# A decoder layer on one Trainium2 core: projection weights in three pieces, a new order of the first block, and another row length for the folded keys

## The chip, the cores and the metric

The kernel runs on 1 core of one Trainium2 chip, as one launch. The metric is the time on the device in microseconds (us); lower is better. The core has TensorE (PE, matrix products, into PSUM banks), VectorE (DVE), ScalarE (ACT), GpSimd (POOL) and SyncE (SP), which here only issues transfers. Each engine takes its own instructions in order, and a semaphore wait holds up all that is behind it on that engine.

## The reference

One pre-norm decoder layer for 8 sequences of 256 tokens of width 256, in float32:

```
x = x + attn(layernorm(x))      # 16 heads of 16, rotary Q and K, causal softmax, W_o
x = x + xattn(layernorm(x))     # 16 heads of 64 over 77 context rows, masked softmax, W_O
x = x + ffn(layernorm(x))       # 256 -> 1024 -> 256, gelu, 8-bit fake-quantised weights + LoRA of rank 16
```

In the cross attention K = ctx @ W_K and Q = xn @ W_Q, and scores = Q K^T / 8. The mask takes context rows out.

## The kernel before, in words

The 8 sequences are blocks 0 to 7. All of the code is unrolled. Each engine has a list of calls written out by hand (`keys(0, 0)`, `project(1, 0)`, ...), which mixes the stages of up to three blocks; the meeting points are semaphores inside the called functions.

Every product with float32 accuracy is made of three matmuls: each operand is split into a high part (ACT copies it to the rounded type) and a low part (raw minus high, on DVE or POOL), and PE makes hi x hi, hi x lo, lo x hi. So each weight passes through a load, `split_hi` on ACT and `split_lo` on DVE or POOL before PE can use it. Each activation passes through PE, ACT and DVE likewise.

Stages of self attention for block a: `statistics_a`, a power on POOL (`inverse_deviation`), `norm_a`, `transpose_a`, `xaT_part` (both halves of the split), `project(a, 0)` and `project(a, 1)` for Q and K, `project_v(a)`, `rotary` on DVE and `rotate` on POOL, `rotated` on ACT, then through DRAM (`store_rotated`, `stacks`) into q_stack and k_stack. `scores(a, g)` for 8 groups of two heads and `maxima` on DVE find each row's maximum. It is transposed (`transpose_max`, `maxima` on ACT into mnegT) and stored by SP (`shifts(a, half)`) into two rows of q_stack, so that `shifted(a, g)` gives scores less the maximum. `exponentials`, `causal` on POOL, `weigh`, `turn_a`, `turn_back_a`, `output_a` follow. Groups 4 to 7 need `shifts(a, 1)`.

Cross attention doesn't make Q. In the prologue the kernel folds W_Q into the keys of all 8 blocks at once: for m = 0 to 7 (two heads each) `keys(m, half)` makes the keys (PE, then ACT and DVE split them, then PE goes on), `fold_keys(m, k, half)` multiplies them with W_Q^T, ACT and DVE copy the result to `stage[m % 2]`, and `store_fold(m)` writes it to `fold_dram` with two transfers of 616 KB. `values2(t, half)` makes the values of all blocks, which POOL stores to v2_dram. Later, for each block b and each group g of four heads, `load_fold(b, g)` brings 308 KB back, ACT and POOL split it (`fold_hi`, `fold_lo`), and `scores2(b, g)` uses it. There are two slots, so a load waits for the scores2 of two groups before.

Before: `fold_dram` is [block, group, k, 128, 308]. A store writes, for each of 128 partitions and 8 blocks, 154 numbers (616 bytes) in one run. A load reads 256 rows of 308 numbers (1232 bytes).

The start: POOL fills the constants, v_aug, k_stack and `work` (ones), all ahead of the first power, and `shift_rows` on SP waits for them all (const_ok 8) ahead of the loads of W_K, ctx and W_Q. W_q, W_k and W_v of self attention are loaded by three transfers and split as one.

Of the kernel before, what the change touches and what calls it, by code (L numbers as in the profile page):

```python
# [21 lines left out]
P = 128  # L22
# [16 lines left out]
def decoder_layer(nc, x, ctxT, mask, wqT, wkT, wvT, woT, wQT, wK, wV, wO, wfcT, bfc, Afc, BfcT,  # L39
# [24 lines left out]
    with ExitStack() as ctx:  # L64
# [111 lines left out]
        fold_dram = nc.dram_tensor("fold_dram", [NB, H // GH, KD, P, GW], F32, kind="Internal").ap()  # L176
# [7 lines left out]
        trig_ld, const_ld, const_ok, ones_ld = sem("trig_ld"), sem("const_ld"), sem("const_ok"), sem("ones_ld")  # L184
        weights = ("qkv", "ctx", "wk", "wv", "wo", "fc", "pj", "wo2", "wq")
# [60 lines left out]
        RAW_DMAS = [3, 1, 1, 1, 1, 1, 1, 1, 1]  # L246
# [13 lines left out]
        def _(sp):  # L260
# [3 lines left out]
            def weight(k):  # L264
                if k == QKV_W:
                    load_raw(sp, k, *[(tiles(k, 3 * D)[:, :, j * D:(j + 1) * D], rows(w))
                                      for j, w in enumerate((wqT, wkT, wvT))])
                elif k == FC_W:
# [28 lines left out]
            def store_fold(m):  # L297
# [3 lines left out]
                for k in range(KD):  # L301
                    sp.dma_start(fold_dram[:, g, k, :, c * 2 * S2:(c + 1) * 2 * S2].rearrange("b p n -> p b n"),
# [59 lines left out]
            def load_fold(b, g):  # L362
# [48 lines left out]
            weight(WO2_W)  # L411
            stacks(1, 0)
            lora_columns()
            stacks(1, 1)
            load_fold(0, 2)
            context_values(0)
            load_fold(0, 3)
            store_rotated(2)
            load_fold(1, 0)
            weight(FC_W)  # L420
            residual_input(1)
            load_x(3)
            biases()
            shifts(1, 0)
            load_fold(1, 1)
            shifts(1, 1)
            stacks(2, 0)
            load_mask(1)
            stacks(2, 1)
            store_rotated(3)  # L430
            residual_input(2)
            load_x(4)
            shifts(2, 0)
            load_fold(1, 2)
            context_values(1)
            load_fold(1, 3)
            load_mask(2)
# [69 lines left out]
        def _(pool):  # L507
            pool.memset(ident[:], 0.0)
# [31 lines left out]
            def split_lo(k):  # L540
                pool.wait_ge(w_hi[k], 1)
# [253 lines left out]
        def _(pe):  # L795
# [79 lines left out]
            def transpose_a(a):  # L875
                if isinstance(a, int) and a == 0:
                    pe.wait_ge(const_ok, 7)
# [2145 lines left out]
```

## Time and profile before

| | us |
|---|---|
| median of 3 timed runs | 632.96 |
| the runs | 632.96, 637.38, 631.59 |
| the profiled execution | 640.39 |
| its span | 638.6 |
| PE busy | 528.9 (83% of the span) |
| DVE, ACT, POOL busy | 394.3, 301.3, 249.0 |

The rows further down are of the profiled execution. Times in them are us from the start of the span, unless marked ns.

### The profile page before, as it was taken

How to read it: one execution, taken by the hardware profiler on the slowest of the kernel's cores; microseconds unless marked ns; L12 is line 12 of the kernel's file. 1: busy time of each engine (PE TensorE's matmuls, PEld its weight loads, DVE VectorE, ACT ScalarE, POOL GpSimd, SP SyncE). 2: the span in 40 equal slices, each digit the busy share in tenths (PEclk: the TensorE clock that was granted, in tenths of full speed). 3: DMA queues.
4: the chain of work that ended last, by engine and by line, in shares of the span. 5: the costliest groups of instructions: out<-in, count | busy, mean ns of one | idle time of the engine just before them, and what ended most of it. 6: DMA issues, size and time to landing. Idle time of an engine off the chain costs nothing.

```text
span 638.6 us, 11817 instructions
## 1 busy us (share of the span) xinstructions
PE 528.9 (83%) x4334; PEld 449.0 (70%) x4334; DVE 394.3 (62%) x1093; ACT 301.3 (47%) x484; POOL 249.0 (39%) x317
## 2 busy tenths in 40 slices
PE   2488779877987889889988997899899899957955
PEld 2376666665867767878778776878887687846755
DVE  4657622488867963796388548954983683554332
ACT  2323344432362765166535654663556277426323
POOL 5820021455256355155252526272465016522210
PEclk9779986987797999999999999999999999989969
DMA  5598997966040414051315232325140601111000
GB/s 186 167 233 174 193 216 143 225 218 205 26 100 1 150 34 121 1 160 52 88 49 147 61 83 72 89 60 118 37 112 19 157 22 42 37 41 38 1 16 17
DMA packets 63709, 62.45 MB, mean 98 GB/s; under 512 B 6868, under 2 KB 60804, under 8 KB 63652
## 3 DMA queue, kind: packets, MB, share of 16 engines
q1 hardware_dynamic: 62148, 56.74, 34.8%
q0 software_dynamic: 1504, 4.95, 2.2%
q8 instruction: 35, 0.57, 0.4%
q14 instruction: 22, 0.18, 0.1%
HBM read 38.28 MB, written 23.10 MB: 96 GB/s over the span
## 4 chain that ended last, share of the span: by engine, by line
PE 54%; DVE 23%; ACT 8%; issue 5%; DMA 5%; POOL 3%; SPq 1%; DVEq 0%; ACTq 0%; POOLq 0%
PE banks L798 9%; PE banks L799 8%; PE banks L800 8%; PE banks L958 5%; DVE banks L2382 4%; PE banks L1049 4%; PE banks L1060 4%; PE banks L935 4%; PE banks L1122 2%; DMA x_in<-in_x 2%; PE banks L972 2%; ACT probs L1752 2%; DMA fold_raw<-fold_dram 2%; DVE hid_lo L2337 2%; PE banks L832 1%
## 5 line engine op out<-in xcount | busy, mean ns | idle before, releaser
L2382 DVE CUSTOM_DVE_ANT_0 banks<-banks,causal_qk 128x256 f32<-128x256 f32 (+1 forms) x256 | 84.1, 388 | 13.0 <-PE banks L935 11.2
L582 POOL TENSOR_SCALAR_AFFINE_SELECT probs<-probs 128x256 f32<-128x256 f32 x128 | 52.2, 435 | 70.1 <-ACT probs L1752 70.1
L565 POOL TENSOR_TENSOR work<-work,rc 128x616 f32<-128x616 f32 x32 | 40.5, 1266 | 99.7 <-DVE rc L2482 99.7
L1752 ACT ACTIVATE probs<-banks 128x768 f32<-128x768 f32 x64 | 51.7, 808 | 32.5 <-PE banks L958 31.8
L1720 ACT ACTIVATE work<-banks 77x512 f32<-77x512 f32 (+1 forms) x72 | 43.2, 600 | 48.4 <-PE banks L1049 44.0
L572 POOL TENSOR_TENSOR fold_lo<-fold_raw,fold_hi 128x616 fp32r<-128x616 f32 x32 | 48.6, 1523 | 43.4 <-ACT fold_hi L1720 43.4
L2480 DVE TENSOR_REDUCE sm<-work 128x8 f32<-128x616 f32 x32 | 25.4, 793 | 51.0 <-ACT work L1782 50.9
L935 PE MATMUL banks<-k_stack,q_stack 96*128 96x256 f32 (+1 forms) x256 | 42.0, 288 | 13.0 <-DVE mneg L2382 9.7
L958 PE MATMUL banks<-q_stack,k_stack 100*128 100x128 f32 (+1 forms) x256 | 47.1, 309 | 5.7 <-DMA q_stack<-mnegT 2.7
L935 PEld LDWEIGHTS banks<-k_stack,q_stack 96*128 96x128 f32 x256 | 36.2, 197 | 20.2 <-DVE mneg L2382 11.6
L2337 DVE TENSOR_TENSOR late<-banks,late 128x512 fp32r<-128x512 f32 x40 | 27.4, 684 | 35.0 <-ACT late L1720 35.0
L1122 PE MATMUL banks<-late,wfc_hi 128*128 128x256 f32 x256 | 42.4, 296 | 6.6 <-DVE up_x L2337 3.4
L798 PE MATMUL banks<-fold_hi,xbT_hi 128*128 128x308 f32 x128 | 47.7, 372 | 0.0
L958 PEld LDWEIGHTS banks<-q_stack,k_stack 100*128 100x128 f32 x256 | 35.9, 201 | 15.2 <-ACT probs L1752 7.5
L1049 PE MATMUL banks<-ident,work 128*77 128x128 f32 x256 | 41.0, 284 | 6.6 <-ACT work L1720 3.0
L1720 ACT ACTIVATE late<-banks 128x512 fp32r<-128x512 f32 x40 | 23.8, 595 | 41.3 <-PE banks L1060 25.5
L1810 ACT ACTIVATE wfc_raw<-banks,bfc_t,wscale 128x256 f32<-128x256 f32 x64 | 32.0, 561 | 20.5 <-DVE hid_lo L2337 15.1
L1122 PEld LDWEIGHTS banks<-late,wfc_hi 128*128 128x128 f32 x256 | 36.1, 197 | 7.7 <-DVE up_x L2337 4.2
L799 PE MATMUL banks<-fold_lo,xbT_hi 128*128 128x308 f32 x128 | 40.1, 314 | 0.0
L800 PE MATMUL banks<-fold_hi,xbT_lo 128*128 128x308 f32 x128 | 39.9, 312 | 0.0
L798 PE MATMUL banks<-wo_hi,late 128*128 128x256 f32 x128 | 39.4, 308 | 0.2 <-DVE late L2337 0.2
L798 PE MATMUL banks<-wpj_hi,hid_hi 128*128 128x256 f32 x128 | 37.7, 295 | 1.8 <-ACT wfc_raw L1810 1.0
(190 smaller groups left out, 1574.7 us busy)
## 6 DMA issues: line engine op xcount, KB each, us to landing
fold_raw<-fold_dram SPq DMA_DIRECT2D x32, 308.0 KB, 3.1
fold_dram<-work SPq DMA_DIRECT2D x8, 616.0 KB, 8.5
rot_dram<-rot_s_hi SPq DMA_DIRECT2D x16, 256.0 KB, 3.0
rot_dram<-rot_s_lo SPq DMA_DIRECT2D x16, 256.0 KB, 2.8
q_stack<-rot_dram SPq DMA_DIRECT2D x32, 128.0 KB, 2.7
k_stack<-rot_dram SPq DMA_DIRECT2D x32, 128.0 KB, 3.0
fold_dram<-fold_raw SPq DMA_DIRECT2D x4, 616.0 KB, 6.1
fold_dram<-fold_raw_hi SPq DMA_DIRECT2D x4, 616.0 KB, 8.4
```

Of the source, the lines that this page charges most:

```text
L572: pool.tensor_tensor(fold[1][:, :, g % 2], raw[:, :, g % 2], fold[0][:, :, g % 2].bitcast(F32), ALU.subtract).then_inc(g_lo, 1)
L582: last = pool.affine_select(out=diagonal, in_=diagonal, compare_op=ALU.is_ge, fill=0.0, base=0, pattern=[[0, 2], [1, P]], channel_multipli ...
L798: pe.matmul(dst, w[0], x_[0], start=first, stop=False, **kw)
L799: pe.matmul(dst, w[0], x_[1], start=False, stop=False, **kw)
L800: return pe.matmul(dst, w[1], x_[0], start=False, stop=last, **kw)
L935: mm = pe.matmul(halves(banks[p])[:, 1 - q, 0:keys_q], q_stack[0:BOTH, g, q * P:(q + 1) * P], k_stack[0:BOTH, g, p, 0:keys_q], start=(q == ...
L958: mm = pe.matmul(halves(p)[:, 1 - k, k * P:T], k_stack[0:SX, g, p, k * P:(k + 1) * P], q_stack[0:SX, g, k * P:T], start=(k == 1), stop=(k ...
L1049: mm = pe.transpose(bank[0:S2, 5, p * T + q * P:p * T + (q + 1) * P], sc2[g % 2][:, q, 2 * c + p, :], ident[:])
L1122: pe.matmul(dst, wfc[0][:, k, m * P:(m + 1) * P], xfT[piece][:, k, :], start=(k == 0 and piece == 0), stop=False)
L1720: act.activation(dst, src, ACT.Copy).then_inc(done, 1)
L1752: act.activation(probs[:, n:n + 2, :], bank[:, 0:2, P:4 * P], ACT.Exp, scale=SCALE).then_inc(p_ok, 1)
L2382: last = dve.tensor_tensor_reduce(out=held[:, at], in0=held[:, at], in1=bias, scale=-1.0, scalar=HUGE, op0=ALU.add, op1=ALU.min, accum_out ...
```

## The change

1. W_q, W_k, W_v of self attention: three transfers with a semaphore each (qkv_ld), split piece by piece (`projection_hi` on ACT, `projection_lo` on DVE); `project(0, 0)`, `project(0, 1)` and `project_v(0)` wait for one, two and three pieces.
2. POOL's fills: half_a comes first, then ident, the causal mask and half of k_stack. The other half, the ones (now 2 partitions) and v_aug come behind the first power, with semaphores of their own. `shift_rows` waits for these, and stands behind the load of W_Q. The low part of W_Q moves from POOL to DVE.
3. `fold_dram` is [group, k, 128, c, block, 154]: a store writes one run of 4928 bytes for each partition, a load reads 512 rows of 616 bytes with two transfers.
4. New orders on all engines, up to about the middle of block 1.

```diff
-        fold_dram = nc.dram_tensor("fold_dram", [NB, H // GH, KD, P, GW], F32, kind="Internal").ap()
+        fold_dram = nc.dram_tensor("fold_dram", [H // GH, KD, P, 2, NB, 2 * S2], F32, kind="Internal").ap()
...
+            def projection(j):
+                sp.dma_start(tiles(QKV_W, 3 * D)[:, :, j * D:(j + 1) * D],
+                             rows((wqT, wkT, wvT)[j])).then_inc(qkv_ld[j], 16)
+
             def shift_rows():
-                sp.wait_ge(const_ok, 8)
+                sp.wait_ge(stack_zero, 2)
+                sp.wait_ge(ones_set, 1)
...
                 for k in range(KD):
-                    sp.dma_start(fold_dram[:, g, k, :, c * 2 * S2:(c + 1) * 2 * S2].rearrange("b p n -> p b n"),
+                    sp.dma_start(fold_dram[g, k, :, c],
                                  stage[m % 2][k].rearrange("p b a s -> p b (a s)")).then_inc(fold_st[m % 2], 16)
...
-                sp.dma_start(raws["fold"][:].rearrange("p (k g n) -> p k g n", k=KD, n=GW)[:, :, g % 2],
-                             fold_dram[b, g].rearrange("k p n -> p k n")).then_inc(g_ld[g], 16)
+                to = raws["fold"][:].rearrange("p (k g c n) -> p k g c n", k=KD, g=2, c=2)[:, :, g % 2]
+                for k in range(KD):
+                    sp.dma_start(to[:, k], fold_dram[g, k, :, :, b]).then_inc(g_ld[g], 16)
...
             first_input()
-            weight(QKV_W)
+            projection(0)
+            projection(1)
+            projection(2)
             trig_tables()
-            shift_rows()
+            load_x(1)
             weight(WK_W)
             weight(CTX_W)
-            load_x(1)
             weight(WQ_W)
+            shift_rows()
+            weight(WV_W)
             store_rotated(0)
+            weight(WO_W)
             stacks(0, 0)
+            store_fold(0)
             stacks(0, 1)
-            weight(WV_W)
-            residual_input(0)
-            weight(WO_W)
-            load_mask(0)
-            store_fold(0)
             store_fold(1)
             store_fold(2)
+            residual_input(0)
             load_x(2)
             shifts(0, 0)
             store_fold(3)
             store_fold(4)
+            shifts(0, 1)
             store_fold(5)
-            shifts(0, 1)
+            store_fold(6)
             store_rotated(1)
-            store_fold(6)
             store_fold(7)
             weight(PJ_W)
+            load_mask(0)
             load_fold(0, 0)
+            weight(WO2_W)
+            lora_columns()
+            weight(FC_W)
+            biases()
             load_fold(0, 1)
...
             pool.tensor_copy(ident_bf[:], ident[:]).then_inc(const_ok, 1)
-            pool.memset(half_a[:], -0.5)
-            pool.memset(v_aug[:], 0.0).then_inc(const_ok, 1)
-            pool.wait_ge(const_ok, 5)
-            pool.memset(v_aug[:, :, :, DH:DH + 1], 1.0).then_inc(const_ok, 1)
-            pool.memset(k_stack[:].bitcast(F32), 0.0).then_inc(const_ok, 1)
-
-            pool.memset(work[:, 0:HH * T], 1.0).then_inc(const_ok, 1)
+            pool.memset(k_stack[:, 0:HH // 2].bitcast(F32), 0.0).then_inc(stack_zero, 1)
+
+            def stack_rest():
+
+                pool.wait_ge(xn_a_ok, 1)
+                pool.memset(k_stack[:, HH // 2:HH].bitcast(F32), 0.0).then_inc(stack_zero, 1)
+
+            def value_constants():
+                pool.memset(v_aug[:], 0.0).then_inc(v_set, 1)
+                pool.wait_ge(v_set, 1)
+                pool.memset(v_aug[:, :, :, DH:DH + 1], 1.0).then_inc(v_set, 1)
+
+            def ones_rows():
+                pool.memset(work[0:2, 0:HH * T], 1.0).then_inc(ones_set, 1)
...
             inverse_deviation(rs_a, lna_ve, lna_rs, 0)
+            stack_rest()
+            ones_rows()
+            value_constants()
             rotate(0, 0)
             rotate(0, 1)
             inverse_deviation(rs_a, lna_ve, lna_rs, 1)
-            split_lo(WQ_W)
...
             project(0, 1)
             keys(0, 0)
             project_v(0)
+            keys(0, 1)
+            fold_keys(0, 0, 0)
+            fold_keys(0, 0, 1)
             transpose_a(1)
-            keys(0, 1)
-            project(1, 0)
-            fold_keys(0, 0, 0)
-            project(1, 1)
-            fold_keys(0, 0, 1)
             fold_keys(0, 1, 0)
             fold_keys(0, 1, 1)
             keys(1, 0)
-            scores(0, 0, 2)
+            project(1, 0)
             keys(1, 1)
-            scores(0, 1, 2)
             fold_keys(1, 0, 0)
             fold_keys(1, 0, 1)
             fold_keys(1, 1, 0)
-            scores(0, 2, 2)
+            project(1, 1)
             fold_keys(1, 1, 1)
             keys(2, 0)
+            scores(0, 0, 2)
+            scores(0, 1, 2)
...
             scores2(0, 0)
             scores(1, 0, 3)
             scores(1, 1, 3)
+            scores(1, 2, 3)
+            scores(1, 3, 3)
+            scores(1, 4, 3)
+            transpose_max(1, 0)
+            spread_largest(1)
             scores2(0, 1)
...
             statistics_a(0)
+            projection_lo(0)
             norm_a(0)
-            split_lo(QKV_W)
             xaT_part(0)
+            projection_lo(1)
+            projection_lo(2)
             rotary(0, 0)
             split_lo(WK_W)
+            split_lo(CTX_W)
             rotary(0, 1)
             statistics_a(1)
-            split_lo(CTX_W)
             keys(0, 0)
+            split_lo(WQ_W)
             norm_a(1)
-            xaT_part(1)
-            rotary(1, 0)
             keys(0, 1)
             fold_keys(0, 0)
```

## Rows read from the trace of the kernel before

**Rows 1.** The page, the span in 40 slices: PE, and its granted clock in tenths

```profile
PE   2488779877987889889988997899899899957955
PEclk9779986987797999999999999999999999989969
```

**Rows 2.** Windows: busy us (x instructions) of each engine, granted clock, DMA share, GB/s

```profile
50.00:57.00 7.00, 5.78 (x46) 4.56 (x44) 5.26 (x25) 2.23 (x4) 0.00 (x0) 1.00 0.76 179
90.20:106.40 16.20, 15.52 (x84) 11.58 (x85) 4.35 (x4) 7.10 (x9) 3.06 (x8) 0.50 0.71 165
200.00:260.00 60.00, 54.84 (x476) 47.68 (x475) 39.81 (x122) 33.92 (x54) 24.92 (x34) 0.95 0.29 81
```

**Rows 3.** Timeline, 3 to 13 us: start, duration, engine, line, operation, idle before

```profile
3.33 3.51 POOL L521 MEMSET k_stack<- 128x4096 f32 x1
4.83 3.77 DVE L2325 TENSOR_SCALAR rs_a<-mv_a 128x2 f32<-128x2 f32 x1
6.82 1.48 ACT L1694 ACTIVATE wqkv_hi<-wqkv_raw 128x1536 fp32r<-128x1536 f32 x1 [4.74 <-DMA wqkv_raw<-in_wvT]
9.52 0.74 DVE L2332 TENSOR_SCALAR xn_a<-x_in,mv_a,rs_a 128x256 f32<-128x256 f32 x2 [0.92 <-POOL rs_a L561]
10.17 1.75 DVE L2256 TENSOR_TENSOR wqkv_lo<-wqkv_raw,wqkv_hi 128x1536 fp32r<-128x1536 f32 x1
...
12.95 0.55 PE L798 MATMUL banks<-xaT_hi,wqkv_hi 128*128 128x256 f32 x1 [1.46 <-DVE xaT_lo L2337]
```

**Rows 4.** Timeline, 10 to 34 us

```profile
10.17 0.41 SPq L251 DMA_DIRECT2D hid_raw<-in_wK  x1
17.15 2.29 DVE L2256 TENSOR_TENSOR hid_lo<-hid_raw,hid_hi 128x2048 fp32r<-128x2048 f32 x1
24.82 0.62 PE L798 MATMUL banks<-late,hid_hi 128*128 128x308 f32 x1 [6.51 <-DVE late L2256]
28.00 4.53 POOL L542 TENSOR_TENSOR wpj_lo<-wpj_raw,wpj_hi 128x2048 fp32r<-128x2048 f32 x1
28.55 4.45 DVE L2332 TENSOR_SCALAR xn_a<-x_in,mv_a,rs_a 128x256 f32<-128x256 f32 x2
33.06 1.12 PE L885 MATMUL banks<-ident,xn_a 128*128 128x128 f32 x4 [4.17 <-DVE xn_a L2332]
```

**Rows 5.** Timeline of PE: a score group, and the first matmul of keys(2,0)

```profile
48.82 0.68 PE L935 MATMUL banks<-k_stack,q_stack 96*128 96x256 f32 x4
...
50.04 0.41 PE L798 MATMUL banks<-late,hid_hi 128*128 128x308 f32 x1
```

**Rows 6.** Timeline of SP, then of PE, 79 to 91 us

```profile
79.45 2.40 SPq L302 DMA_DIRECT2D fold_dram<-work  x2
81.98 1.88 SPq L354 DMA_DIRECT2D q_stack<-mnegT  x2
...
90.18 1.23 PE L958 MATMUL banks<-q_stack,k_stack 100*128 100x128 f32 x4 [2.68 <-DMA q_stack<-mnegT]
```

**Rows 7.** DMA views: issues (median us to landing), then SP's queue, 40:100 and 0:40

```profile
fold_raw<-fold_dram SPq DMA_DIRECT2D x32, 308.0 KB, 3.1
fold_dram<-work SPq DMA_DIRECT2D x8, 616.0 KB, 8.5
late_raw<-in_ctxT SPq DMA_DIRECT2D x1, 616.0 KB, 6.1
...
q1 hardware_dynamic: 16988, 11.52, 88.1%
q1 hardware_dynamic: 6208, 7.20, 62.7%
```

**Rows 8.** Waits of ACT (total, times, longest), and one piece of the chain

```profile
ACT fold_hi L1720 <- DMA fold_raw<-fold_dram: 9.2, 9, 2.6
...
238.51 3.09 DMA fold_raw<-fold_dram
```

**Rows 9.** Timeline of DVE, block 1

```profile
151.07 4.19 DVE L2393 CAST mneg_s<-mneg 128x16 fp32r<-128x16 f32 x1
```

More of the change, by code:

```diff
@@ L264, in weight @@
             def weight(k):
[L265 to L268, printed above, removed]
+                if k == FC_W:
                     sp.wait_ge(vx_ps, 2 * VT)
@@ L431, in _ @@
             residual_input(2)
+            load_fold(1, 2)
+            load_fold(1, 3)
             load_x(4)
             shifts(2, 0)
-            load_fold(1, 2)
+            load_mask(2)
             context_values(1)
-            load_fold(1, 3)
-            load_mask(2)
             load_fold(2, 0)
@@ L541, in split_lo @@
                 pool.wait_ge(w_hi[k], 1)
+                if k == WQ_W:
+                    pool.wait_ge(xn_a_ok, 2)
                 pool.tensor_tensor(split_to[k][1], raw_of[k], split_to[k][0].bitcast(F32),
@@ L897, in project @@
                         pe.wait_ge(v_ok, a)
+                elif isinstance(a, int) and a == 0:
+                    pe.wait_ge(w_lo[QKV_W], 2)
                 for j in range(2):
@@ L907, in project_v @@
                 pe.wait_ge(trig, 2 * a + 1)
+                if isinstance(a, int) and a == 0:
+                    pe.wait_ge(w_lo[QKV_W], 3)
                 for q in range(QT):
@@ L1187, in _ @@
             fold_keys(4, 1, 1)
+            scores(0, 6, 2)
             keys(5, 0)
-            transpose_max(0, 1)
-            shifted(0, 0)
+            scores(0, 7, 2)
             keys(5, 1)
@@ L1196, in _ @@
             keys(6, 0)
+            transpose_max(0, 1)
+            shifted(0, 0)
+            keys(6, 1)
+            fold_keys(6, 0, 0)
             shifted(0, 1)
-            keys(6, 1)
-            shifted(0, 2)
-            fold_keys(6, 0, 0)
             fold_keys(6, 0, 1)
             fold_keys(6, 1, 0)
-            shifted(0, 3)
+            shifted(0, 2)
             fold_keys(6, 1, 1)
             keys(7, 0)
+            shifted(0, 3)
             weigh(0, 0)
+            keys(7, 1)
+            fold_keys(7, 0, 0)
             shifted(0, 4)
-            keys(7, 1)
-            shifted(0, 5)
-            fold_keys(7, 0, 0)
             fold_keys(7, 0, 1)
             fold_keys(7, 1, 0)
+            shifted(0, 5)
+            fold_keys(7, 1, 1)
             weigh(0, 1)
             shifted(0, 6)
-            fold_keys(7, 1, 1)
             weigh(0, 2)
+            values2(0, 0)
             shifted(0, 7)
-            values2(0, 0)
             values2(0, 1)
-            weigh(0, 3)
             values2(1, 0)
             values2(1, 1)
-            turn_a(0)
             values2(2, 0)
             values2(2, 1)
-            turn_back_a(0)
             values2(3, 0)
             values2(3, 1)
+            weigh(0, 3)
             values2(4, 0)
+            turn_a(0)
             values2(4, 1)
+            turn_back_a(0)
             transpose_a(2)
@@ L1243, in _ @@
             lora_down(0)
-            scores(1, 2, 3)
             transpose2(0, 0, 1)
-            scores(1, 3, 3)
             weigh2(0, 0)
@@ L1728, in values @@
                 act.wait_ge(v_ps, a + 1)
+                if isinstance(a, int) and a == 0:
+                    act.wait_ge(v_set, 2)
                 act.wait_ge(pv_ps, 4 * a)
@@ L1822, in _ @@
             rotated(0, 0)
-            rotated(0, 1)
             split_hi(WQ_W)
             keys(0, 0)
+            rotated(0, 1)
+            keys(0, 1)
+            fold_keys(0, 0)
             values(0)
             xaT_part(1)
-            keys(0, 1)
-            fold_keys(0, 0)
-            rotated(1, 0)
             fold_keys(0, 1)
@@ L2257, in split_lo, with projection_lo @@
                                   ALU.subtract).then_inc(w_lo[k], 1)
+            def projection_lo(j):
+                cols = slice(j * D, (j + 1) * D)
+                dve.wait_ge(w_hi[QKV_W], j + 1)
+                low(wqkv[1][:, :, cols], tiles(QKV_W, 3 * D)[:, :, cols], wqkv[0][:, :, cols], w_lo[QKV_W])
             def largest(n, k):
@@ L2563, in _ @@
             keys(7, 0)
-            mask_bias(0)
-            norm_a(2)
             keys(7, 1)
@@ L2569, in _ @@
             split_lo(WV_W)
+            mask_bias(0)
+            norm_a(2)
             attention(0)
+            split_lo(WO_W)
             attention_lo(0)
-            split_lo(WO_W)
             largest(1, PJ_W)
@@ L2600, in _ @@
             maxima(1, 8)
+            softmax2(0, 0)
+            scale(1, PJ_W)
+            sums2(0, 0)
+            quantise(1, PJ_W, 0)
+            softmax2(0, 1)
+            quantise(1, PJ_W, 1)
+            add_lora(1, PJ_W, 0)
             maxima(1, 9)
+            sums2(0, 1)
+            add_lora(1, PJ_W, 1)
+            context_lo(0, 0)
             maxima(1, 10)
```

157 lines of the change are left out of this document (75 added, 82 removed).

## Prediction

> **What bounds the kernel now.** I read the page's slices first. TensorE (PE) is busy nine tenths or so from the middle of the run on, and clearly less in the first third; its granted clock is below full in three stretches there [rows 1]. Each slice is 16 us. The windows say the same in numbers: one block's worth of steady state, 200 to 260 us, has 54.84 us of PE work in 60 us at a clock of 0.95, whereas 90.2 to 106.4 us is just as full, but at half clock, 1.2 of 2.4 GHz [rows 2]. The steady state is left alone by the change but for its fold loads, so the gain or loss sits in the prologue, up to about 134 us, and in 28 later loads. Adding up the idle stretches of PE in the timeline of 0 to 134 us, three stand out: the start up to the first projection (12.95 us) [rows 3], the waits ahead of keys(0,0) and of the second block's transposes [rows 4], and the wait for the shift rows at 90.18 us [rows 6].
>
> The profiled execution took 640.39 us (span 638.6 us and 1.8 around it), 7.4 above the median of 632.96. The three timed runs spread over 5.8 us. I make the sum against the profiled execution, then say what carries over.
>
> **Part 1: first input to first projection.** x is there at 3.65 us. The tiny VectorE (DVE) instruction on rs_a that starts at 4.83 takes 3.77 us, and it ends when GpSimd's (POOL's) fills end [rows 3]. POOL then takes the power, and the normalisation, the transposes and the split put project(0,0) at 12.95. In the changed kernel only the four small constants and half the k_stack fill (3.51 / 2 = 1.8 us, started about 2.3) lie ahead, so POOL is free at 4.1. The power is done by about 5.9. The first weight piece is the second transfer of the run; ACT waited until 6.82 for the third piece, and I put the first at 5. Then its high part costs a third of ScalarE's (ACT's) 1.48 us, its low part a third of 1.75 us [rows 3]. So normalisation is at 6.2, transposes at 7, project(0,0) at 9.8: 3.1 us earlier. The remaining fills move behind xn_a_ok and take 1.8 (second half of k_stack), 1.8 (ones) and 1.1 (v_aug) us on POOL, over at 11.7; the first rotation needs POOL only about 13.5, so they cost nothing. If the first rotation came 2 us sooner, they would cost that.
>
> **Part 2: keys(0,0).** wK is issued at 10.17, behind shift_rows, which waits for the fills [rows 4]. Now it goes out behind load_x(1), which waits for the normalisation, at about 7.5. It needs some 6 us to land, then ACT 1.9 us and DVE 2.29 us, then the low part of ctx, 1232 columns to 2048, 1.4 us. rotary(0,1) and statistics_a(1), an estimated 2.8 us together, stood before that last one on DVE and go behind it. That gives keys(0,0) at 18.5 to 19.5 in place of 24.82, so 5.3 to 6.3 us earlier (3.1 of them from part 1).
>
> **Part 3: the second block.** POOL's low part of wQ takes 4.53 us, and the DVE normalisation that starts beside it takes 4.45 us in place of 0.74 [rows 3, 4]; PE is idle 4.17 us before 33.06 [rows 4]. The split goes to DVE, 2.3 us at the rate of hid_lo [rows 4]. That removes the 4.2 us, but norm_a(1) now waits for POOL's power behind rotate(0,1), and keys(0,1) of DVE is queued behind both; fold_keys(0,0,1) on PE needs it. I count a new wait of about 2 us. project(1,0) and project(1,1) come later in PE's order, with no change in work. Walking the orders through with these durations, keys(2,0) is at about 41.5 in place of 50.04 [rows 5]. At that point the old order has done three score groups that the new has not, at 0.6 us each (the one at 48.82 took 0.68) [rows 5]. So parts 1 to 3 bring 8.5 - 1.8 = 6.7 us. Bounds: 3 (the keys, copy, subtract loop holds PE back anyway; it leaves PE 1.2 us idle in the 7 us of m = 2 [rows 2]) and 9.5 (less half-clock time in the first 39 us).
>
> **Part 4: the shift rows.** SyncE (SP) issued the shifts of half 1 at 81.98, right behind store_fold(5), whose data came only at 79.45, and PE waited 2.68 us for them [rows 6]. Now shifts(0,1) stands ahead of store_fold(5), behind store_fold(4), which is long ready. This wait goes: 2.7 us. What is late next is the ordinary loop through ACT, no more than 0.8 us. After the wait the granted clock is 0.50 until 106.4: 15.52 us of PE work, of which full clock would save at most half, 7.8 us [rows 2]. The DVE and ACT work between would eat an estimated 2.8 of it, which leaves 5.
>
> **Part 5: rows of the fold store.** 16 stores of 616 KB were written in rows of 616 bytes; they fill the DMA engines (88.1% from 40 to 100 us, 16988 packets) [rows 7]. That is 0.881 x 960 / 16988 = 50 ns of an engine per packet of 680 bytes. From 0 to 40 us packets of 1160 bytes take 0.627 x 640 / 6208 = 65 ns [rows 7]. Long rows cost less per byte. With 4928 bytes the stores land sooner (8.5 us now [rows 7]), perhaps in 4 to 5, but PE waits for none in the trace once the shifts are out from behind them: 0 us. Price if that cover is gone: none, it only gets better.
>
> **Part 6: rows of the fold load.** 32 loads of 308 KB in 256 packets of 1232 bytes become 64 DMAs and 512 packets of 616 bytes. Per engine: 16 x 65 ns = 1.0 us becomes 32 x 50 ns = 1.6 us, and the second issue is 0.4 us behind the first (SP takes 0.41 for one [rows 4]), mostly beside the transfer. So each load lands 0.6 to 1.0 us later than 3.1 us [rows 7]. ACT waited for a load 9 times, 9.2 us in all, and the chain that ended last runs through three of them (one shown) [rows 8]. At 0.8 us: 3 x 0.8 = 2.4 if only these count, 9 x 0.8 = 7.2 if all do. I take 3. The 32 further issues are 0.4 us each of SP, spread over 450 us, where SP mostly waits: nothing.
>
> What the row length may not do: the Trainium skill, page "DMA: Bandwidth & Descriptors", section "Specifications", states that line rate is reached from 512 bytes per transfer. By that rule neither 616 nor 1232 nor 4928 bytes would matter. The 616 KB of ctx, in rows of 2464 bytes, landed in 6.1 us against 8.5 for a fold store [rows 7], which leans against it, though the queues differed in depth.
>
> **Part 7: the move of block 1.** In the new order the first five score groups of block 1 run ahead of scores2(0,1), FC_W is loaded earlier, and SP waits at it for the end of values2, with load_fold(0,1) and both stacks(1) behind. By my walk the stacks land 2 us before PE reaches scores(1,0). The 4.19 us that DVE lost on a tiny cast beside POOL's split of wO [rows 9] are likely lost again, on quantise, since that split stays on POOL. Context values are loaded behind load_fold(0,3) and may hold weigh2(0,0) for 1 us. In sum 0, between -3 and +4.
>
> **The sum.** 640.4 - 6.7 - 2.7 - 5 + 3 = 629.0 for an execution like the profiled one. The profiled one lies 7.4 above the median, about what one slow-clock stretch costs, so I take the median run as one in which that stretch is mostly absent, and count 1 us of part 4's 5. 632.96 - 6.7 - 2.7 - 1 + 3 = **625.5**.
>
> **Rivals.**
> (a) The load rows cost nothing. Each load's awaited end is set by its latency, and the extra 0.6 us of packets lies in the gaps; the chain's three pieces stay as long as they are. Then 622.5. The rule above would give just this. For it: the DMA share in steady state is 0.29 [rows 2]. Against: packets do take engine time, above.
> (b) The slow-clock stretch is in the median run as well, and goes. 632.96 - 6.7 - 2.7 - 5 + 3 = 621.5, and with (a) 618.5. For it: PEclk is low behind each long idle stretch of PE in the prologue [rows 1, 4, 6]. Against: the 7.4 us.
> (c) What the start gains is given back in the fold phase, where from 45 to 88 us each m needs its own loop PE, ACT, DVE, and the moved score groups and the second block's projections leave more unfilled gaps. Then only 2 us of the 6.7 arrive: 630 to 631. For it: from 50 to 57 us PE is busy 5.78 us of 7 and DVE 5.26 [rows 2], so a chain between them, and no one engine, sets the pace. Against: the work left over is the same.
> (d) Slower. fold_hi stands at the head of ACT's queue, and behind it stand exponentials and copies that PE waits for. If a load in short rows lands 2 us later in place of 0.8 (its two DMAs queue behind stacks or x), and the nine waits all reach PE, it costs 18 us against gains of 10.4: 640.5. It decides from 10.4 / 9 = 1.2 us per load.
> (e) The change doesn't do what it says: the short rows are merged or the long ones cut, so that DMA is as before. Then parts 1 to 4 stay, as in (a).
>
> **How the numbers follow.** Forecast as summed (621 to 630): 0.40. (a), (e) and (b), 617 to 623: 0.30. (c): 0.22. (d): 0.08. A measurement tells 1% (6.3 us) from no change; the border to faster is 626.6. Of the forecast's 0.40, six tenths lie below it: 0.24 + 0.30 = 0.54 faster; 0.38 within 1%; 0.08 slower. The range takes in (b) with the good end of part 3 (632.96 - 9.5 - 2.7 - 5 + 1 = 617, and 3 less for part 7) and (c) with the bad end of part 7: 613 to 636.
>
> **What would show it.** rs_a short and project(0,0) near 10 us; keys(0,0) near 19; norm_a(1) under 1 us; no wait on mnegT in shifted(0,4); clock at full from 40 to 120 us; fold stores landing in 5 us or less; fold loads at 3.9 us and ACT's wait for them 12 to 16 us. Wrong it would be if fold loads took over 5 us, if a new stall in the fold phase or in block 1 brought half clock back, or if the start's gain was gone by values2(0,0).

## The result, and the profile after

The changed kernel takes 640.44 us (median of 17 runs, 637.52 to 643.16), the kernel before 633.25 (17 runs, 631.59 to 639.60) in the same sessions. The ratio is 1.0073, with a 95% interval of 1.0048 to 1.0097. So the change costs 4.6 us or so (0.0073 x 633), where the prediction said 625.5 with a range of 613 to 636. The ratio comes from all the runs, while the two medians lie 7.2 us apart: the runs of the kernel before fall into two groups, nine from 631.6 to 633.3 and eight from 636.0 to 639.6, and their median is the last of the lower group. Here and below a median is that of all runs of a kernel, and a ratio leaves out the few runs that are more than 1.5% above the fastest of their kernel. The profiled execution of the changed kernel has a span of 638.0 us and a mean clock of 0.946.

The page's slices of the changed kernel, PE and its granted clock, which answer to [rows 1]:

```profile
PE   4488888469879799889889997999999899948955
PEclk9799989867998999999999998999999899988979
```

The clock of 6 has left the seventh slice (96 to 112 us), and a new low stretch stands in the eighth to tenth, 112 to 160 us; PE fills the eighth and ninth to four and six tenths only. The windows of the same kernel, in the columns of [rows 2]:

```profile
90.20:106.40 16.20, 16.20 (x91) 12.52 (x90) 2.00 (x6) 7.59 (x13) 2.17 (x3) 0.99 0.38 117
120.00:130.00 10.00, 3.33 (x13) 2.79 (x13) 3.54 (x21) 1.95 (x3) 5.74 (x6) 0.57 1.06 294
130.00:140.00 10.00, 7.06 (x30) 5.70 (x30) 8.19 (x28) 0.72 (x1) 3.62 (x4) 0.58 0.28 91
200.00:260.00 60.00, 51.76 (x459) 44.52 (x459) 38.71 (x122) 31.81 (x52) 24.07 (x33) 0.97 0.30 81
```

From 200 to 260 us PE now gets through 459 matmul instructions in place of 476 and is busy 51.76 us in place of 54.84, at no lower clock: the steady state has got slower as well. (The busy time alone would not show it: r6 below, with rows of 1232 bytes in its loads, is busy 52.33 us there and gets through 476.) The start went about as forecast. Timeline of 4 to 34 us, changed kernel, for [rows 3] and [rows 4]:

```profile
4.75 0.17 DVE L2361 TENSOR_SCALAR rs_a<-mv_a 128x2 f32<-128x2 f32 x1
6.29 0.73 DVE L2368 TENSOR_SCALAR xn_a<-x_in,mv_a,rs_a 128x256 f32<-128x256 f32 x2
9.71 0.55 PE L816 MATMUL banks<-xaT_hi,wqkv_hi 128*128 128x256 f32 x1 [1.46 <-ACT xaT_hi L1747]
...
21.78 0.62 PE L816 MATMUL banks<-late,hid_hi 128*128 128x308 f32 x1 [6.61 <-DVE late L2287]
...
28.93 0.73 DVE L2368 TENSOR_SCALAR xn_a<-x_in,mv_a,rs_a 128x256 f32<-128x256 f32 x2 [1.90 <-POOL rs_a L577]
30.11 0.41 PE L850 MATMUL banks<-wo_hi,wpj_hi 64*128 64x308 f32 x2 [2.24 <-DVE wo_lo L2373]
```

rs_a takes 0.17 us in place of 3.77, project(0,0) starts at 9.71 (12.95 before), keys(0,0) at 21.78 (24.82), the blocked normalisation is down from 4.45 to 0.73, and the new wait that was put at 2 us is 2.24.

Then block 1. Timeline of SP, 106 to 117 us (first and last of the 16 stack transfers shown), and of PE, ACT, POOL and DVE behind it:

```profile
106.09 0.38 SPq L252 DMA_DIRECT2D wfc_raw<-in_wfcT  x1
...
107.57 1.19 SPq L376 DMA_DIRECT2D fold_raw<-fold_dram  x2
108.94 0.46 SPq L340 DMA_DIRECT2D q_stack<-rot_dram  x1
...
116.51 0.44 SPq L343 DMA_DIRECT2D k_stack<-rot_dram  x1
...
124.09 1.11 PE L957 MATMUL banks<-k_stack,q_stack 96*128 96x256 f32 x4 [4.89 <-DMA k_stack<-rot_dram]
128.00 0.72 ACT L1747 ACTIVATE fold_hi<-fold_raw 128x616 fp32r<-128x616 f32 x1 [5.47 <-DMA fold_raw<-fold_dram]
...
139.32 4.51 POOL L558 TENSOR_TENSOR wo_lo<-wo_raw,wo_hi 128x2048 fp32r<-128x2048 f32 x1
140.46 4.45 DVE L2316 TENSOR_SCALAR wpj_raw<-wpj_raw,wscale 128x2048 f32<-128x2048 f32 x1
145.09 1.86 PE L1082 MATMUL banks<-work,v 77*32 77x256 f32 x16 [3.38 <-DMA v<-v_dram]
```

The stacks, which scores(1,0) needs, are issued from 108.94 to 116.5, behind W_fc, which SP held until values2 was done: SP issues nothing between 93.17 and 106.09 us. PE waits 4.89 us for them, ACT 5.47 for the next fold load, and then PE waits 3.38 for the context values.

The waits view, ACT for fold loads (in total, times, longest), for [rows 8], and the fold lines of the page's DMA issues, for [rows 7]:

```profile
ACT fold_hi L1747 <- DMA fold_raw<-fold_dram: 19.3, 11, 5.5
...
fold_raw<-fold_dram SPq DMA_DIRECT2D x64, 154.0 KB, 2.8
fold_dram<-work SPq DMA_DIRECT2D x8, 616.0 KB, 4.0
```

The waits have doubled, from 9.2 us [rows 8]. The stores land in 4.0 us in place of 8.5 [rows 7]. The chain that ended last runs through seven fold loads, where before it ran through three.

**Where the time went.** The profiled execution of before contained a half-clock stretch, and at 640.39 us it lies above all 17 timed runs of that kernel. A better partner is the profiled execution of run r3 (below), a kernel that is as fast as the one before; this execution lacks the stretch. At 632.46 us it is on the fast side of r3's own runs (median 636.26), and the changed kernel's, at 639.70, is near its median, so the two are 7.2 us apart where the ratio says 4.6. Landmarks of PE in each, timeline; first transpose_b of block 0, then turn_a of block 1 and the last transposes of the feed-forward part. Run r3:

```profile
122.01 0.66 PE L1015 MATMUL banks<-ident,work 128*128 128x128 f32 x4 [0.48 <-DVE work L2333]
...
181.09 1.09 PE L985 MATMUL banks<-ident,rot 128*128 128x128 f32 x8 [0.72 <-ACT rot L1721]
...
605.67 1.12 PE L1091 MATMUL banks<-ident,late_raw 128*128 128x128 f32 x4 [4.54 <-DVE late_raw L2333]
```

The changed kernel:

```profile
114.90 0.60 PE L1036 MATMUL banks<-ident,work 128*128 128x128 f32 x4
...
180.10 1.09 PE L1006 MATMUL banks<-ident,rot 128*128 128x128 f32 x8 [0.72 <-ACT rot L1747]
...
612.84 1.11 PE L1112 MATMUL banks<-ident,late_raw 128*128 128x128 f32 x4 [4.54 <-DVE late_raw L2368]
```

And the first landmark in the profiled execution of before:

```profile
130.46 0.66 PE L1014 MATMUL banks<-ident,work 128*128 128x128 f32 x4 [0.48 <-DVE work L2332]
```

The changed kernel is 7.1 us ahead of r3 at the first landmark, 1.0 ahead at the second, and 7.2 behind at the third. So in these two traces 7.1 were gained in the prologue, 6.1 given back in block 1, and 8.2 lost in the steady state. The experiments take these three apart.

### The profile page after: what moved, and what is told of

Same layout as the page of the kernel before. It is cut to its first block, busy times and chain, and to the rows that moved or that the text cites. A ratio compares the mean times of both kernels' runs of the same rounds, so it can differ in the third digit from the quotient of the medians.

```text
span 638.0 us, 11856 instructions
## 1 busy us (share of the span) xinstructions
PE 527.0 (83%) x4334; PEld 447.4 (70%) x4334; DVE 389.8 (61%) x1096; ACT 301.9 (47%) x486; POOL 245.1 (38%) x317
## 4 chain that ended last, share of the span: by engine, by line
PE 56%; DVE 15%; DMA 8%; ACT 8%; issue 6%; POOL 3%; SPq 3%; DVEq 0%; ACTq 0%; POOLq 0%
PE banks L816 9%; PE banks L817 8%; PE banks L818 8%; PE banks L980 4%; PE banks L1082 4%; PE banks L957 4%; DMA fold_raw<-fold_dram 3%; PE banks L1071 3%; DVE banks L2418 3%; PE banks L1144 3%; PE banks L850 2%; PE banks L994 2%; ACT probs L1781 2%; DMA k_stack<-rot_dram 2%; PE banks L1050 2%
## 5 line engine op out<-in xcount | busy, mean ns | idle before, releaser
L598 POOL TENSOR_SCALAR_AFFINE_SELECT probs<-probs 128x256 f32<-128x256 f32 x128 | 53.7, 446 | 64.1 <-ACT probs L1781 64.1
L1144 PE MATMUL banks<-late,wfc_hi 128*128 128x256 f32 x256 | 44.5, 306 | 8.7 <-ACT wfc_raw L1839 5.1
L816 PE MATMUL banks<-fold_hi,xbT_hi 128*128 128x308 f32 x128 | 49.5, 387 | 0.0
L980 PE MATMUL banks<-q_stack,k_stack 100*128 100x128 f32 (+1 forms) x256 | 45.1, 299 | 5.3 <-ACT probs L1781 4.4
L1144 PEld LDWEIGHTS banks<-late,wfc_hi 128*128 128x128 f32 x256 | 38.0, 207 | 10.0 <-ACT wfc_raw L1839 5.6
L980 PEld LDWEIGHTS banks<-q_stack,k_stack 100*128 100x128 f32 x256 | 34.1, 192 | 15.3 <-ACT probs L1781 10.3
L1839 ACT ACTIVATE wfc_raw<-banks,bfc_t,wscale 128x256 f32<-128x256 f32 x64 | 32.0, 561 | 20.3 <-DVE hid_lo L2373 14.5
L817 PE MATMUL banks<-fold_lo,xbT_hi 128*128 128x308 f32 x128 | 41.5, 324 | 0.0
L818 PE MATMUL banks<-fold_hi,xbT_lo 128*128 128x308 f32 x128 | 41.3, 322 | 0.0
L1082 PE MATMUL banks<-work,v 77*32 77x256 f32 x512 | 35.0, 391 | 6.1 <-DMA v<-v_dram 6.0
L572 POOL TENSOR_TENSOR rot_s_lo<-rot,rot_s_hi 128x512 fp32r<-128x512 f32 x16 | 22.7, 1418 | 44.0 <-ACT rot_s_hi L1747 44.0
```

What stands on the lines that cost most here:

```text
L598: last = pool.affine_select(out=diagonal, in_=diagonal, compare_op=ALU.is_ge, fill=0.0, base=0, pattern=[[0, 2], [1, P]], channel_multipli ...
L816: pe.matmul(dst, w[0], x_[0], start=first, stop=False, **kw)
L817: pe.matmul(dst, w[0], x_[1], start=False, stop=False, **kw)
L818: return pe.matmul(dst, w[1], x_[0], start=False, stop=last, **kw)
L980: mm = pe.matmul(halves(p)[:, 1 - k, k * P:T], k_stack[0:SX, g, p, k * P:(k + 1) * P], q_stack[0:SX, g, k * P:T], start=(k == 1), stop=(k ...
L1082: mm = pe.matmul(halves(5)[32 * j:32 * j + 32, c, :], v2[:, col:col + 32], p2T[:, 2 * c + j // 2, :], start=True, stop=True, skip_group_ch ...
```

## The experiments

Each run has its own times of the kernel before beside it: 634.96 us (29 runs) for r1 to r4, 635.54 (23) for r5 to r8, 636.79 (28) for r9 to r11, 636.22 (17) for r12. Ratios are to these, with 95% intervals.

**r1, before with the new rows alone.** This is the third part of the change, and no other.

```diff
-fold_dram = nc.dram_tensor("fold_dram", [NB, H // GH, KD, P, GW], ...)
+fold_dram = nc.dram_tensor("fold_dram", [H // GH, KD, P, 2, NB, 2 * S2], ...)
...
-    sp.dma_start(fold_dram[:, g, k, :, c * 2 * S2:(c + 1) * 2 * S2].rearrange("b p n -> p b n"),
+    sp.dma_start(fold_dram[g, k, :, c],
...
-    sp.dma_start(...[:, :, g % 2], fold_dram[b, g].rearrange("k p n -> p k n"))
+    for k in range(KD):
+        sp.dma_start(to[:, k], fold_dram[g, k, :, :, b])
```

> The kernel before with nothing but the new row length: stores of 4928-byte rows, loads of 616-byte rows by two transfers. Theory L (the short rows of the fold load cost most of the loss: each load later by 0.6 to 1.4 us, ACT's wait for them 9 to 19 us): 637 to 641 us against 633 of before. Theory B (the loss comes from the new order of block 1 and the loads are harmless): 631 to 634, or less if the stores' relief removes the wait for the shift rows.

Measured 640.98 us, 1.0101 (1.0063 to 1.0140). The rows alone are as slow as the whole change.

**r2, the changed kernel with the old rows.** The same lines the other way round, in the changed kernel.

> The changed kernel with the old row length, stores in 616-byte rows and loads in 1232-byte rows by one transfer. Theory L: 628 to 633, that is 7 to 12 below the changed kernel. Theory B: 638 to 641, as the changed kernel.

Measured 638.39 us, 1.0055 (1.0025 to 1.0085). The new order alone is still slower than before, so the rows are not the whole cause; against the changed kernel (1.0073) it isn't told apart, as Theory B expected. What the short rows of the loads cost and what the long rows of the stores bring nearly cancel here, as r5 and the landmarks below show. With short store rows PE was held up in the fold phase: the timeline of PE and ACT shows ACT waiting for the stage buffer to be stored.

```profile
69.95 0.69 ACT L1746 ACTIVATE work<-banks 128x616 f32<-128x616 f32 x1 [2.81 <-DMA fold_dram<-work]
...
70.78 0.62 PE L849 MATMUL banks<-wo_hi,wpj_hi 64*128 64x308 f32 x2 [2.39 <-ACT work L1746]
```

**r3, before with two transfers for each load.** The rows stay at 1232 bytes; only the number of transfers doubles.

```diff
-    sp.dma_start(...[:, :, g % 2], fold_dram[b, g].rearrange("k p n -> p k n"))
+    for k in range(KD):
+        sp.dma_start(to[:, k], fold_dram[b, g, k])
```

> The kernel before with each fold load made of two transfers of 1232-byte rows, rows as before. If the second issue is what makes loads late, 636 to 640, as with short rows; if the row length is, 633 to 634.

Measured 636.26 us, 0.9999 (0.9972 to 1.0025). Two transfers instead of one cost nothing; the length of the rows does. ACT's waits for fold loads in r3, then in r1:

```profile
ACT fold_hi L1721 <- DMA fold_raw<-fold_dram: 6.4, 8, 2.0
```

```profile
ACT fold_hi L1721 <- DMA fold_raw<-fold_dram: 15.2, 11, 4.1
```

One load in each, timeline of SP and ACT. r3, 1232 bytes:

```profile
503.97 0.80 SPq L373 DMA_DIRECT2D fold_raw<-fold_dram  x2
...
506.70 0.72 ACT L1721 ACTIVATE fold_hi<-fold_raw 128x616 fp32r<-128x616 f32 x1 [0.86 <-DMA fold_raw<-fold_dram]
```

r1, 616 bytes:

```profile
507.78 1.19 SPq L373 DMA_DIRECT2D fold_raw<-fold_dram  x2
...
511.18 0.72 ACT L1721 ACTIVATE fold_hi<-fold_raw 128x616 fp32r<-128x616 f32 x1 [1.53 <-DMA fold_raw<-fold_dram]
```

From issue to use it is 2.73 us with long rows and 3.40 with short ones. Of the 0.67 us, 0.39 lies in SP's two issues (1.19 against 0.80). Over the whole run the waits differ by 15.2 - 6.4 = 8.8 us; r1's ratio less r3's, 0.0102, is 6.5 us.

**r4, the changed kernel with W_fc and the biases behind both stacks on SP.**

```diff
             lora_columns()
-            weight(FC_W)
-            biases()
             load_fold(0, 1)
             stacks(1, 0)
             stacks(1, 1)
+            weight(FC_W)
+            biases()
```

> The changed kernel with the load of W_fc and the biases put behind both halves of block 1's stacks on SyncE. Theory B: PE's wait of 4.9 us for k_stack goes, the clock stays up behind it, and the time falls by 5 to 9 us, to 632 to 636. Theory L: the stacks then wait less, but the gain is given back in later waits; within 2 us of the changed kernel.

Measured 634.20 us, 0.9982 (0.9947 to 1.0017), 0.0091 or 5.8 us below the changed kernel. The wait for the stacks is gone in the timeline of PE. Of the five score groups the first two run at full clock (0.65 us each, against 1.11 in the changed kernel), the three from 121.56 us on take 1.12 again:

```profile
118.50 0.65 PE L957 MATMUL banks<-k_stack,q_stack 96*128 96x256 f32 x4 [0.19 <-issue]
```

So the low clock of block 1 is mostly still there: r4's windows have 0.50 from 126 to 136 us. What went is the wait, and PE's wait for the context values is down from 3.38 to 1.43 us.

**r5, r4 with each load in one transfer of 1232-byte rows, out of the long-row store.** A load reads two neighbouring blocks' halves, so scores2 works from wrong keys in r5 and in r6; the amount of data and of work is the same.

```diff
+                at = min(b, NB - 2)
+                sp.dma_start(...[:, :, g % 2],
+                             fold_dram[g, :, :, 0, at:at + 2].rearrange("k p b n -> p k (b n)"))
```

> As the changed kernel with W_fc's load behind the stacks, long store rows kept, but each fold load is one transfer of 256 rows of 1232 bytes. In this layout those bytes belong to two neighbouring blocks, so the cross attention is computed from wrong keys; all times and sizes are as in the full kernel. Theory L' (the 616-byte rows of the loads cost about 8 us of steady state, since loads land later; stores in long rows help): 8 us under the 634 of the same kernel with short load rows, 625 to 628. Theory P (two loads' issue or something else in the order): 632 to 634.

Measured 625.76 us, 0.9857 (0.9805 to 0.9908). Against r4 that is 0.0125, or 7.9 us, for loads in one transfer of long rows in place of two of short rows; by r3 the number of transfers alone costs nothing. ACT's waits in r5:

```profile
ACT fold_hi L1747 <- DMA fold_raw<-fold_dram: 7.0, 6, 2.1
```

In r4 they were 14.5 us in 10 waits: 7.5 us less waiting, 7.9 us less time.

**r6, the same loads in r1.** The order of before, long-row stores, 1232-byte loads.

> The kernel before with long store rows and loads of 1232-byte rows by one transfer; keys are wrong as above. If the store rows matter in the old order, because half 1's shifts queue behind a store, the executions at 636 to 640 with the clock lowered behind that wait go, and the median is 631 to 633; if not, it is 635 as before. Theory L' says in any case 7 to 9 under the 641 of the same kernel with short load rows.

Measured 635.91 us, 1.0017 (0.9983 to 1.0051), 0.0084 or 5.3 us below r1. In the old order the rows of the stores are worth nothing that can be measured: they land in 3.5 us in place of 8.5 in before, and the time is that of before.

**r7, r4's order with a third layout.** A store writes runs of 616 bytes that lie 1232 apart, a load reads rows of 1232 bytes.

```diff
+fold_dram = nc.dram_tensor("fold_dram", [H // GH, KD, P, NB, GW], ...)
...
+    sp.dma_start(fold_dram[g, k, :, :, c * 2 * S2:(c + 1) * 2 * S2],
...
+    sp.dma_start(...[:, :, g % 2], fold_dram[g, :, :, b].rearrange("k p n -> p k n"))
```

> W_fc's load behind the stacks, and a third layout, group, k, partition, block, 308 numbers: stores of 616-byte runs that lie 1232 apart, loads of 1232-byte rows by one transfer; the result is the full one. If the length of a run is what counts in a store, the stores take 6 to 8 us and the stage waits of the old rows come back, 630 to 634; if it is that the pieces lie far apart, they take 4 us and the time is 626 to 628.

Measured 629.84 us, 0.9891 (0.9850 to 0.9932). ACT waits 2.31 us for a stage buffer at 68.56 us, and the stores land in 6.4 us.

**r8, r4's order with the layout of before**, and **r12, the same kernel once more**.

> W_fc's load behind the stacks, and the old layout throughout. Against the third layout it tells whether the distance of the runs matters. Theory L' with slow stores: 630 to 634, as the third layout; ACT waits 2 to 3 us for a fold store in the fold phase and the clock falls behind it in part of the executions.

Measured 629.21 us, 0.9885 (0.9827 to 0.9942, six runs).

> The base of the last three runs once more, since its 629.2 us (0.9885) rested on six runs and two kernels that should hardly differ from it gave 0.993 and 0.995. If the base's first figure stands (0.9885 again, about 628), then W_Q's split on POOL, the late shift rows and the early context values cost 5, 3 and 4 us. The rival: the first figure was a low draw and the base lies near 0.992; then the late shifts and the early values are worth nothing that can be measured and W_Q's split on POOL costs about 2 to 3 us.

Measured 631.42 us, 0.9916 (0.9879 to 0.9954, twelve runs): between the two expectations. I take the mean of both, 0.990, as this base. r7 gives the same, so how far apart the short runs lie is not what matters. r7, r8 and r12 beat the kernel before by about 1%, and the changed kernel by 1.7%. r2 is this base with W_fc ahead of the stacks, as in the changed kernel, and it is at 1.0055: a second pair, like r4 and the changed kernel, in which W_fc's place costs time, here 0.0155 or 9.8 us.

**r9, that base with W_Q's low part back on POOL.**

```diff
 # POOL
             inverse_deviation(rs_a, lna_ve, lna_rs, 1)
+            split_lo(WQ_W)
 # DVE
             keys(0, 0)
-            split_lo(WQ_W)
             norm_a(1)
```

> The changed kernel with W_fc and the biases behind both stacks of block 1 and the old rows of the folded keys (that base measured 629.2 us, 0.9885 of the kernel before), but with the low part of W_Q made by POOL again, behind the power of block 1, as in the kernel before. By part 3 of the prediction the move of this split to DVE takes away 4.2 us of a blocked normalisation and puts back a wait of 2 us, so this kernel should be 2 us slower than its base: about 631.4 (0.992 of before), and the trace should show norm_a(1) on DVE lasting 3 to 4.5 us beside POOL's split. The rival: the first product with W_Q waits for the low part of W_Q in either order, and what norm_a(1) loses is hidden behind it: within 1 us of 629.2.

Measured 634.86 us, 0.9962 (0.9926 to 0.9999): 0.0062 or 4 us above the base, with intervals that overlap (r12's ends at 0.9954). The direction is that of part 3; the size isn't settled. The timeline of r9:

```profile
24.35 4.50 POOL L555 TENSOR_TENSOR wpj_lo<-wpj_raw,wpj_hi 128x2048 fp32r<-128x2048 f32 x1
24.50 4.83 DVE L2366 TENSOR_SCALAR xn_a<-x_in,mv_a,rs_a 128x256 f32<-128x256 f32 x2 [2.38 <-POOL rs_a L574]
29.00 0.63 PE L848 MATMUL banks<-wo_hi,wpj_hi 64*128 64x308 f32 x2 [4.59 <-POOL wpj_lo L555]
```

DVE is blocked beside POOL once more (forecast 3 to 4.5 us), and PE waits 4.59 us for the split itself.

**r10, the base with the second shifts behind store_fold(5).**

```diff
             store_fold(4)
-            shifts(0, 1)
             store_fold(5)
+            shifts(0, 1)
```

> The same base (629.2 us, 0.9885 of before), but with shifts(0, 1) behind store_fold(5) on SP, as in the kernel before. By part 4 of the prediction PE then waits 2.7 us for the shift rows, and a stretch at half clock follows: 632 (0.993) if only the wait comes back, up to 637 with the stretch. The rival: in most executions of the kernel before SP had the shift rows out early enough, and only the profiled one waited; then the place of the two transfers is worth nothing: within 1 us of 629.2, and no wait on mnegT in the trace.

Measured 632.72 us, 0.9934 (0.9905 to 0.9963), not told apart from the base; PE has no wait on the shift rows in its trace. SP issued them early, at 74.01 us, since the store ahead of them was ready. The rival stands.

**r11, the base with the context values ahead of load_fold(0, 3).**

> The same base (629.2 us, 0.9885 of before), but with the context values of block 0 loaded ahead of load_fold(0, 3). In the changed kernel weigh2(0,0) waited 3.4 us for the values, and 1.4 with W_fc moved. If PE's wait there reaches the end, 628 (0.987). The rival: load_fold(0,3) goes out later by as much and ACT meets it late, so nothing changes: within 1 us of 629.2.

Measured 634.49 us, 0.9949 (0.9917 to 0.9981): no gain. PE's wait for the context values at the first weigh2 is gone in its trace (2.02 us in r12), so taking this wait away doesn't shorten the run. Whether it is worse than the base by up to 3 us was not settled.

**The landmarks in all the profiled executions.** The three landmarks of above can be read in every trace. The first column is the start of the first transpose_b of block 0, the second the time from there to turn_a of block 1, the third from there to the last transposes of the feed-forward part, all in us:

| | first landmark | block 1 | steady state |
|---|---|---|---|
| before | 130.5 | 58.8 | 424.5 |
| old order without the wait: r3, r1, r6 | 122.0, 121.2, 121.7 | 59.1, 58.8, 59.0 | 424.6, 433.0, 429.4 |
| changed kernel | 114.9 | 65.2 | 432.7 |
| r2: as that, short store rows, long load rows | 124.6 | 65.3 | 428.7 |
| r4: W_fc behind the stacks | 114.0 | 59.4 | 432.1 |
| r5: as r4, long load rows | 114.0 | 58.3 | 423.9 |
| r7 to r12: as r5, short store rows, each with its edit | 121.1 to 124.8 | 58.4 to 59.1 | 423.9 to 428.3 |

Each cell is a single execution, but the groups stand apart. In the new order the first landmark is at 114 to 115 us with long store rows (three traces) and at 121 to 125 with short ones (seven). Block 1 takes 65 us in the two kernels with W_fc ahead of the stacks and 58 to 59 in the twelve others. The steady state takes 432 to 433 us in the three traces with load rows of 616 bytes and 424 to 429 in the eleven others.

## Why the prediction was wrong

The terms of the sum, with what the runs give for each (a ratio's difference times 635 us):

| | predicted | measured | from |
|---|---|---|---|
| parts 1 to 3, start and second block | -6.7 | -6.3 | r8 and r12 against before, part 4 and the rest of the new order in it |
| part 4, shift rows and the clock behind them | -3.7 | 0 | r10 is 2.2 above the base, within the intervals |
| part 5, store rows | 0 | -2.7 | r5 (0.9857) against the base (0.990), intervals overlap |
| part 6, load rows | +3 | +7.9 | r4 against r5; 5.3 in the old order |
| part 7, block 1 | 0 | +5.8 | changed kernel against r4 |
| sum | -7.4 | +4.7 | |

The measured terms follow one path of kernels, so that they add up to the measured +4.6 says nothing more; each alone is good to some 3 us.

**Parts 1 to 3 held up to keys(2,0), and then depended on part 5.** project(0,0) came 3.2 us sooner against 3.1 forecast, norm_a(1) is short, the new wait is 2.24. keys(0,0) came at 21.78, not at 18.5 to 19.5; the same start gave 19.15 in r12 and 19.59 in r4. keys(2,0) came at 40.14, where 41.5 was forecast and before had 50.04. At the first landmark the changed kernel is 7.1 us ahead of r3, which looks like the 6.7, but the long store rows are in it: with short ones the new order is there at 121.1 to 124.8, no sooner than the old order without its wait, which is there at 121.2 to 122.0. So in these traces the fold phase gave the start's gain back unless the store rows were long. That r8 and r12 are still 1% below before is measured; where they win it, these traces don't show, and that it comes to 6.3 where 6.7 was forecast may be luck.

**Part 4 took a wait of one execution for a wait of all.** The prediction said that the half-clock stretch is mostly absent from the median run, and then kept the 2.7 us wait that stood right before it, at full price. That step failed: the profiles of r1, r3 and r6, all in the old order, have neither the wait (0.2 us in r1) nor the stretch (their clock is 1.00 from 90.2 to 106.4 us), and r10 has no such wait either. Only r3 of the three has short store rows as before has. For the execution it was read from the price was right: 2.7 + 5 = 7.7 us, and before's profile reaches the first landmark 8.5 us behind r3's (130.46 against 122.01). How many runs of before have the wait and the stretch, and whether these are its upper group from 636 us on, no run here shows.

**Part 5 put a term at nothing for a reason that held in the old order only**, "PE waits for none in the trace". The old order (r6) bears it out. In the new order the fold phase starts earlier and its stage buffers come round sooner, and with short-row stores ACT has to wait for them: 2.81 us in r2, 2.31 in r7, 2.18 in r12 at 65 us. No trace with long store rows has such a wait. r12 is still 0.7 us ahead of r4 there (keys(6,0) on PE at 67.00 and 67.73), then it falls behind (keys(7,0) at 78.64 and 75.12) and is 7.0 us behind at the first landmark (121.06 and 114.02). The ratios give only 2.7 us, with overlapping intervals; how much of the 7 arrives at the end is open. The windows of 70 to 90 us show what follows. r12 (short rows), then r4 (long rows):

```profile
70.00:90.00 20.00, 18.47 (x118) 14.23 (x118) 5.63 (x9) 10.28 (x14) 4.50 (x11) 0.64 0.70 180
```

```profile
70.00:90.00 20.00, 16.77 (x145) 12.68 (x146) 7.37 (x9) 11.53 (x16) 7.33 (x15) 0.93 0.79 284
```

r12 has the clock at 0.64 there and gets through 118 matmul instructions, r4 has 0.93 and gets through 145. Over the same 20 us r2, r7, r8 and r10, with short store rows, have 0.58 to 0.63, r9 and r11, also with short ones, 0.87 and 0.93, and the changed kernel and r5, with long ones, 0.93 and 0.91. These are single executions; that the wait for the stage brings the low clock about was not tried by itself.

**Part 6 was mis-sized.** Forecast 3 us, measured 7.9. The lateness was right (0.6 to 1.0 us forecast; 0.67 in the load shown, though 2.2 in the one at 566 us). So was ACT's total, 12 to 16 us: 15.2 in r1, 14.5 in r4. What failed was "I take 3", that only the three waits in the chain count. ACT's extra waiting and the extra time were 7.5 and 7.9 us in r4 against r5, 8.8 and 6.5 in r1 against r3, and the steady state of r4 is 8.2 us longer than r5's: most of it reaches the end, and once loads are late, more of them come into the chain, seven in place of three. The prediction's own upper bound, 9 x 0.8 = 7.2, was the better value.

Here the Trainium skill speaks the other way: the page "DMA: Bandwidth & Descriptors", section "Specifications", has line rate from 512 bytes. Rival (a) rested beside that rule. It fell: 1232-byte rows against 616-byte rows were worth 7.9 and 5.3 us, and the 616 KB stores landed in 3.5 to 4.2 us (medians of the runs) in rows of 4928 bytes and in 6.4 to 8.5 in rows of 616.

**Part 7 was walked wrongly, the largest miss.** It was put at 0, between -3 and +4, and measured 5.8 us. The prediction saw that SP waits at W_fc with load_fold(0,1) and both stacks behind it, and then had the stacks land "2 us before PE reaches scores(1,0)". They landed 4.89 us after. What the walk had wrong, in its start on SP, in PE's speed or in the transfers, isn't told apart: SP came to the stacks only at 108.94, the sixteen issues took nearly 0.5 us each, and the DMA engines were full (share 1.06 from 120 to 130 us). Then came what the text had foreseen: 4.45 us of DVE on quantise beside POOL's split, 3.38 us for the context values where 1 was allowed; and, not foreseen, half clock from 124 to 138 us (0.57 and 0.58 in the two windows above). That W_fc's place causes the loss is shown twice, by r4 against the changed kernel (5.8 us) and by the base against r2 (9.8), and block 1 takes 6 us more in both traces that have W_fc ahead. The low clock isn't the cause by itself, since r4 has most of it too.

**The rivals.** (a) and (e) fell by r1. (b) found no support: by r10 the place of the shift rows is worth 2 us or nothing. (c), the start's gain given back in the fold phase, is what the traces with short store rows look like; in the changed kernel the gain passed the fold phase and was given back in block 1. (d) gave 640.5, which is what was measured, by luck: it had 2 us per load on nine waits and all gains kept; in truth it is 0.7 us for most loads, and the other 6 us are block 1.

## What to carry to other kernels

When a wait is the same kind in many places of an in-order queue, price it at the whole of the view of waits, not at the pieces in the chain: pieces enter the chain as they grow. When a change makes one engine earlier, walk the queues of the others again at the new speed, above all what stands ahead of the next transfer that this engine needs, and price again the transfers that nothing waited for at the old speed; a load that itself waits belongs behind those that are ready. Take a wait from a profiled execution that lies above the median only if a second execution has it.

## What the runs showed of the hardware

- What issuing a load costs SP: two issues of 256 rows of 616 bytes took 1.19 us, two of 128 rows of 1232 bytes 0.80 (r3), one of 256 rows of 1232 bytes 0.38 (r5). So it isn't the number of rows alone; whether it is their length or the shape of the transfer was not tried.
- A fill of 2 partitions by 2048 takes POOL as long as one of 128 partitions: 1.79 us against 1.80. Timeline of POOL, changed kernel:

```profile
7.08 1.80 POOL L529 MEMSET k_stack<- 128x2048 f32 x1 [1.35 <-DVE xn_a L2368]
8.82 1.79 POOL L537 MEMSET work<- 2x2048 f32 x1
```

- The blocking of DVE beside a long POOL subtraction came back in the two places shown, where a DVE instruction on SBUF tiles met one: 4.83 us for a 0.73 us normalisation in r9, 4.45 us in the changed kernel for quantise, which takes 1.23 in r3. A DVE instruction that reads a PSUM bank (`work<-banks,mx` at 139.75) took 0.80 us beside the same subtraction, as everywhere else. The Trainium skill, page "SBUF — State Buffer", section "SBUF: two separate sides", has an exclusive lock on a port pair that the two share, held for the whole instruction; the rows agree, since both DVE instructions last as if they began when POOL's had ended: the normalisation ends 0.48 us behind it (24.50 + 4.83 against 24.35 + 4.50), quantise 1.08 us behind it (140.46 + 4.45 against 139.32 + 4.51).
